# Attention block with projection and feed-forward on one core: weights split ahead of the first rows, the shift rows placed before a store, one GpSimd difference moved, GpSimd's sum added at the next tile, more adds on VectorE in the last item

## The chip, the core and the metric

The kernel runs on one core of one Trainium2 chip. The metric is the device time of one execution in microseconds (us). PE is TensorE, DVE is VectorE, ACT is ScalarE, POOL is GpSimd and SP is SyncE, which here issues every DMA. The engines run their own instruction streams in order and meet at semaphores.

## What is computed

`x` is 2 x 2048 rows of 256 values in float32. Cut to what matters:

```python
def attn(x, W_qkv, W_out):            # H, D = 16, 64
    q, k, v = split(x @ W_qkv, 3)     # 256 -> 3 * 1024
    score = einsum('bihd,bjhd->bijh', q, k) / D ** 0.5      # causal mask
    out = einsum('bijh,bjhd->bihd', softmax(score, over j), v)
    return out.reshape(b, l, H * D) @ W_out                 # 1024 -> 256

x = x + attn(layernorm(x), W_qkv, W_out)
x = x + layernorm(x) @ (W + up_aux @ lora_up @ lora_down @ down_aux).T + b
```

## The kernel before

Products of float32 data are made from a rounded high part and the rest as a low part, so most products are three matmuls (high by high, low by high, high by low). There are three blocks, one after the other.

**Projection** (`project_qkv`, tensors `a_`). Eight tiles of 512 rows. A tile is normalised on DVE (L439), turned by PE (L282), its high part is copied by ACT (`xt_hi`, L405 for the first tile) and its low part taken by DVE (`xt_lo`, L446). PE then makes 24 groups of six matmuls (L304), emptied in turn by ACT and DVE (L359). The weights come in six parts of 512 columns (`w_raw`, loads L209); ACT makes `w_hi` of a part (`high_part`, L381), DVE `w_lo` (`low_part`, L452). Before the first tile parts 0 and 1 are split, after the first rows; the other parts are split between the groups of the first tile. PE starts the first group when part 0 of `w_lo` and `xt_lo` are there.

**Attention** (`attention`, tensors `b_`, `f_`, `g_`). Sixteen items, each two heads of one batch. An item has 40 slots, one for each pair of a query tile t of 512 and a key block j of 128: tile 0 has slots 0 to 3, tile 1 slots 4 to 11, tile 2 slots 12 to 23, tile 3 slots 24 to 39; the last four of a tile lie on the diagonal and are narrower. For a slot, PE makes scores (L839 subtracts the maximum with the rows of `shift`, L843, L851), ACT the exponentials `probs` (L973), PE the product with V (`o_acc`, L908). PE runs two slots ahead with the scores. During item n, PE also makes chunks of scores for item n+1 in a ring of three banks (L872, L880), DVE takes their row maxima (L1047), and near slot 35 turns them into rows (L1060, L1062, semaphore `max_rows_ready`). SP copies these into `shift` with four small DMAs (`place_max`, L782), and PE waits for them at the first scores of item n+1.

The sums of `probs` are split: POOL adds the early j of a tile into `sum_pool` (L1161), DVE the last full one and the diagonal ones into `sum_dve` (L1073, L1077, L1087), and at the end adds `sum_pool` to it (L1093). The table `LATE_FULL` says how many full slots of each tile DVE adds in the last item; in all other items it is one. PE sums over partitions (`denominators`, L920), ACT copies that to `den_row` (L1002), SP moves it (`invert`, L753), DVE inverts it (L1113), SP sends it through memory (L757) and back as `recip` (L761), POOL multiplies (`normalise`, L1146), SP stores (`store_o`, L746). POOL also makes eight low parts of the next item's K and Q per item (`split_diff`, L723) at the slots of the list `LO_SLOTS`, from copies by ACT at slots 0 to 3 (L959, L961).

In the last item there are no chunks. There SP loads the first outputs (`load_first_o`), ACT and DVE split them (`first_high` L995, `first_low` L1107) and the output weights (L989, L1101).

**Output projection and feed-forward** (`project_and_ffn`, tensors `c_`) is not touched.

The order on each engine is written out by hand: the functions `item` of each engine walk through the slots. `late_tile(n, s, previous)` gives the tile that ended just before slot s (s = 0, 4, 12, 24). On SP an item is: load V, invert and store tile 3 of the item before, invert and store tile 0, then for p = 0, 1 a load, invert and store of tile p + 1, then `place_max`.

## Time and profile before

| | us |
|---|---|
| median of 3 runs | 1861.03 |
| lowest and highest run | 1859.17, 1866.96 |
| the profiled execution | 1860.62 |
| its span, from first to last instruction | 1858.8 |
| projection / attention / rest, from the span's start | 0 to 313 / 313 to 1713.7 / to 1858.8 |

In the profile a row of the order in time gives the start in us from the span's start, the length in us, engine, line, operation, output <- inputs, and how many instructions are merged (x4); in brackets stands how long the engine was idle just before and what released it. Rows of waits give: engine, line, what it waited for: us in total, times, longest.

### The profile page before, as it was taken

What the parts mean: (1) busy time and instruction counts of PE and PEld (TensorE: products, weight loads), DVE (VectorE), ACT (ScalarE), POOL (GpSimd) and SP (SyncE); (2) the same over time, 40 slices, a digit from 0 to 9 for tenths busy, and PEclk for the clock granted to TensorE, in tenths of its full rate; (3) what the DMA queues carried; (4) which work ended last, traced back from release to release, by engine and by line L of the source; (5) the groups of instructions that cost most, each with busy time, mean ns of one, the idle gap of its engine ahead of it and who ended that gap; (6) DMA issues with size and microseconds to landing.
All of it is one profiled execution on the core that took longest, in us unless ns stands there. A gap on an engine that the chain in (4) does not pass through costs nothing. (4 is left out here: it accounts for less than half of the span.)

```text
span 1858.8 us, 34889 instructions
## 1 busy us (share of the span) xinstructions
PE 1774.3 (95%) x13720; PEld 1051.1 (57%) x13720; DVE 1243.1 (67%) x2094; ACT 788.2 (42%) x982; POOL 958.7 (52%) x529
## 2 busy tenths in 40 slices
PE   7999999999999999999999999999999999999998
PEld 5878777554545454445454455445454545444897
DVE  5365653767676767676767767676767676756665
ACT  3222114454545454545454454545454545455231
POOL 1011001666665858485766656666667585835211
PEclk9999999999999999999999999999999999999999
DMA  5656446212121212122121222121212121022551
GB/s 209 223 184 233 164 176 215 69 42 75 47 69 48 72 50 69 47 69 73 49 70 47 78 59 78 41 81 36 81 47 70 47 75 47 24 75 92 193 204 57
DMA packets 153858, 171.39 MB, mean 92 GB/s; under 512 B 48202, under 2 KB 94816, under 8 KB 153696
## 3 DMA queue, kind: packets, MB, share of 16 engines
q1 hardware_dynamic: 153696, 169.17, 28.7%
q8 instruction: 110, 1.80, 0.4%
q14 instruction: 52, 0.43, 0.1%
HBM read 97.02 MB, written 71.57 MB: 91 GB/s over the span
## 5 line engine op out<-in xcount | busy, mean ns | idle before, releaser
L1047 DVE TENSOR_REDUCE f_part_max<-b_ring 128x1 f32<-128x512 f32 (+3 forms) x1200 | 675.0, 604 | 289.2 <-PE b_ring L872 193.3
L973 ACT ACTIVATE b_probs<-b_scores 128x1024 f32<-128x1024 f32 (+3 forms) x640 | 564.3, 898 | 604.0 <-PE b_scores L843 343.1
L1161 POOL TENSOR_TENSOR b_sum_pool<-b_sum_pool,b_probs 128x1024 f32<-128x1024 f32 x234 | 558.9, 2388 | 31.8 <-POOL b_sum_pool L1161 0.5
L843 PE MATMUL b_scores<-b_split 64*128 64x512 f32 (+2 forms) x1920 | 296.8, 418 | 0.0
L843 PE MATMUL b_scores<-f_split 64*128 64x512 f32 (+2 forms) x1920 | 295.9, 416 | 0.0
L1161 POOL TENSOR_TENSOR b_sum_pool<-b_probs 128x1024 f32<-128x1024 f32 x48 | 114.6, 2387 | 314.3 <-DVE g_sum_dve L1093 204.4
L908 PE MATMUL b_o_acc<-b_probs,b_v_in 128*64 128x512 f32 (+3 forms) x1280 | 271.2, 545 | 0.0
L908 PE MATMUL b_o_acc<-b_probs,f_v_in 128*64 128x512 f32 (+3 forms) x1280 | 269.0, 541 | 0.0
L843 PEld LDWEIGHTS b_scores<-b_split 64*128 64x128 f32 x1920 | 179.7, 189 | 12.0
L843 PEld LDWEIGHTS b_scores<-f_split 64*128 64x128 f32 x1920 | 179.5, 188 | 11.2
L1087 DVE TENSOR_TENSOR g_sum_dve<-g_sum_dve,b_probs 128x512 f32<-128x512 f32 (+3 forms) x198 | 158.1, 798 | 31.0 <-ACT b_probs L973 26.5
L872 PE MATMUL b_ring<-b_split 64*128 64x512 f32 (+2 forms) x640 | 142.8, 434 | 18.9 <-DVE f_part_max L1047 18.0
L359 DVE COPY a_stage_d<-a_made 128x512 f32<-128x512 f32 x96 | 66.1, 690 | 140.5 <-PE a_made L304 140.4
L359 ACT COPY a_stage_a<-a_made 128x512 f32<-128x512 f32 x96 | 56.4, 587 | 224.6 <-PE a_made L304 222.9
L908 PEld LDWEIGHTS b_o_acc<-b_probs,b_v_in 128*64 128x64 f32 x1280 | 78.2, 137 | 110.4 <-issue 81.5
L872 PE MATMUL b_ring<-f_split 64*128 64x512 f32 (+2 forms) x560 | 125.1, 434 | 16.1 <-DVE f_part_max L1047 15.4
L908 PEld LDWEIGHTS b_o_acc<-b_probs,f_v_in 128*64 128x64 f32 x1280 | 77.6, 136 | 107.9 <-issue 80.5
L872 PEld LDWEIGHTS b_ring<-b_split 64*128 64x128 f32 x640 | 64.7, 183 | 129.1 <-issue 124.6
L839 PE MATMUL b_scores<-b_shift,p_first_rows 64*128 64x512 bf16 (+2 forms) x640 | 117.9, 358 | 10.9 <-ACT b_probs L973 6.6
L839 PE MATMUL b_scores<-f_shift,p_first_rows 64*128 64x512 bf16 (+2 forms) x640 | 117.4, 356 | 9.6 <-ACT b_probs L973 5.3
L872 PEld LDWEIGHTS b_ring<-f_split 64*128 64x128 f32 x560 | 56.7, 184 | 112.2 <-issue 107.7
L723 POOL TENSOR_TENSOR b_split<-f_raw,b_split 128x512 fp32r<-128x512 f32 x64 | 81.4, 1295 | 54.4 <-ACT b_split L959 54.4
(138 smaller groups left out, 2208.8 us busy)
## 6 DMA issues: line engine op xcount, KB each, us to landing
f_raw<-k_t SPq DMA_DIRECT2D x32, 512.0 KB, 4.7
f_raw<-q_t SPq DMA_DIRECT2D x32, 512.0 KB, 5.8
g_recip<-r_t SPq DMA_DIRECT2D x128, 128.0 KB, 2.9
o_t<-g_o_norm SPq DMA_DIRECT2D x64, 256.0 KB, 2.0
q_t<-a_stage_a SPq DMA_DIRECT2D x32, 256.0 KB, 2.4
q_t<-a_stage_d SPq DMA_DIRECT2D x32, 256.0 KB, 2.0
k_t<-a_stage_a SPq DMA_DIRECT2D x32, 256.0 KB, 2.0
k_t<-a_stage_d SPq DMA_DIRECT2D x32, 256.0 KB, 2.0
```

What stands on the lines that cost most here:

```text
L359: copy(stage[e][s][:], made[:, g % BANKS, :]).then_inc(emptied[e], 1)
L723: vec.tensor_tensor(lo[u][:, cols], raw[p][:, which, inner], halves(hi[u][:, cols]), ALU.subtract).then_inc(split_lo, 1)
L839: nc.tensor.matmul(scores[s % 2][:, h, lo:TILE], consts["first_rows"][head(h), :], shift[u][head(h), queries], start=True, stop=False)
L843: last = nc.tensor.matmul(scores[s % 2][:, h, lo:TILE], a[u][head(h), keys], b[u][head(h), queries], start=False, stop=(term == 2 and not ...
L872: last = nc.tensor.matmul(rowwise[h][:, 0:wide], q_hi[u][head(h), ib * P:(ib + 1) * P], k_hi[u][head(h), c * TILE:c * TILE + wide], start= ...
L908: last = nc.tensor.matmul(o_acc[head(h), off:], v_in[u][:, j, head(h)], probs[s % PR][:, h, off:], start=(j == 0), stop=(j == NB * t + NB ...
L973: nc.scalar.activation(probs[s % PR][:, :, off:], scores[s % 2][:, :, off:], ACT.Exp, scale=scale).then_inc(exp_done, 1)
L1047: nc.vector.tensor_reduce(part_max[:, h, ib, c:c + 1], rowwise[h][:, 0:width], AX.X, ALU.max).then_inc(chunk_reduced, 1)
L1087: nc.vector.tensor_tensor(sum_dve[t % 2][:, :, off:], sum_dve[t % 2][:, :, off:], probs[s % PR][:, :, off:], ALU.add).then_inc(dve_added, 1)
L1161: nc.gpsimd.tensor_tensor(sum_pool[:], first, probs[s % PR][:], ALU.add).then_inc(pool_added, 1)
```

## The change

Five edits:

- **First rows.** ACT makes `w_hi` of parts 0 and 1 before `xt_hi` of the first tile, DVE `w_lo` of parts 0 and 1 before `xt_lo`. PE starts the first group at `xt_hi`, and waits for `xt_lo` only ahead of its third matmul.
- **Placing.** `place_max` on SP stands before the store of tile 2 rather than after it.
- **LO_SLOTS.** The second difference moves from slot 8 to 3, the third to fifth from 9, 10, 11 to 8, 9, 10, and the first from 3 to 2.
- **The sum of POOL** (L1093) is issued by DVE at the slot after the tile, ahead of that slot's own add, not behind the last add of the tile.
- **LATE_FULL** goes from (0, 1, 2, 6) to (0, 2, 4, 6): in the last item DVE adds one full slot more of tile 1 and two more of tile 2, and POOL as many less.

```diff
@@ TensorE, group() and tile() of the projection
+                            if first and (g, k) == (0, 2):
+                                pe.wait_ge(xt_lo_ready, 1)
...
-                    pe.wait_ge(xt_lo_ready, T + 1)
+                    if first:
+                        pe.wait_ge(xt_hi_ready, 1)
+                    else:
+                        pe.wait_ge(xt_lo_ready, T + 1)
@@ ScalarE
                 take_root(0, 0)
+                for p in range(2):
+                    high_part(p)
                 act.wait_ge(transposed, 1)
                 nc.scalar.copy(xt_hi[0][:], turned[:]).then_inc(xt_hi_ready, 1)
-                for p in range(2):
-                    high_part(p)
@@ VectorE
                 normalise(0, 0)
+                for p in range(2):
+                    low_part(p)
                 turn(0, 0)
...
-                for p in range(2):
-                    low_part(p)
@@ attention
-    LO_SLOTS = [3, 8, 9, 10, 11, 20, 21, 22]
+    LO_SLOTS = [2, 3, 8, 9, 10, 20, 21, 22]
...
-    LATE_FULL = (0, 1, 2, 6)
+    LATE_FULL = (0, 2, 4, 6)
@@ SyncE
                         invert(n, p + 1)
+                        if following and p == LOADS - 1:
+                            place_max(n + 1, 1 - u)
                         store_o(n, (pair, u), p + 1)
-                    if following:
-                        place_max(n + 1, 1 - u)
@@ VectorE
-                    if d == NB - 1 and first_dve(n, t) < NB * t:
-
-                        dve.wait_ge(dve_added, dve_before[n, s] + 1)
-                        dve.wait_ge(pool_added, pool_done[n, t])
-                        nc.vector.tensor_tensor(sum_dve[t % 2][:], sum_dve[t % 2][:], sum_pool[:], ALU.add
-                                                ).then_inc(dve_added, 1)
+                def add_pool_sum(n, t):
+
+                    dve.wait_ge(dve_added, sum_ready[n, t] - 1)
+                    dve.wait_ge(pool_added, pool_done[n, t])
+                    nc.vector.tensor_tensor(sum_dve[t % 2][:], sum_dve[t % 2][:], sum_pool[:], ALU.add).then_inc(dve_added, 1)
...
+                        for late in late_tile(n, s, previous):
+                            if late[1]:
+                                add_pool_sum(*late)
                         if dve_adds(n, s):
                             add_unit(n, s)
```

What the change moves is seen in the order of instructions. Names in it are output<-inputs; [waits ...] are the semaphores. First ACT at the start of the program, before and now:

```order
2 L370 ACTIVATE a_root<-a_var_eps 128x4 [waits a_var_ready]
3 L405 CAST a_xt_hi<-a_turned 128x1024 [waits a_transposed]
4 L381 CAST a_w_hi<-a_w_raw 128x2x512 [waits a_w_loaded0]
5 L381 CAST a_w_hi<-a_w_raw 128x2x512 [waits a_w_loaded1]
6 L381 CAST a_w_hi<-a_w_raw 128x2x512 [waits a_w_loaded2]
```

```order
2 L375 ACTIVATE a_root<-a_var_eps 128x4 [waits a_var_ready]
3 L386 CAST a_w_hi<-a_w_raw 128x2x512 [waits a_w_loaded0]
4 L386 CAST a_w_hi<-a_w_raw 128x2x512 [waits a_w_loaded1]
5 L412 CAST a_xt_hi<-a_turned 128x1024 [waits a_transposed]
6 L386 CAST a_w_hi<-a_w_raw 128x2x512 [waits a_w_loaded2]
```

Two parts of the weights moved ahead of the first rows; on DVE the same two parts moved ahead of `xt_lo`.

Then SP near the end of the first item, from the loads of `recip` for tile 2 on, before and now:

```order
239 L761 DMA g_recip<-r_t 64x512 [waits g_inverse_stored,g_o_stored]
240 L761 DMA g_recip<-r_t 64x512
241 L746 DMA o_t<-g_o_norm 128x512 [waits g_o_ready,g_o_stored]
242 L782 DMA b_shift<-f_max_high 1x16x128 [waits f_max_rows_ready,f_shift_cleared]
243 L782 DMA b_shift<-f_max_low 1x16x128
```

```order
239 L766 DMA g_recip<-r_t 64x512 [waits g_inverse_stored,g_o_stored]
240 L766 DMA g_recip<-r_t 64x512
241 L787 DMA b_shift<-f_max_high 1x16x128 [waits f_max_rows_ready,f_shift_cleared]
242 L787 DMA b_shift<-f_max_low 1x16x128
243 L787 DMA b_shift<-f_max_high 1x16x128
244 L787 DMA b_shift<-f_max_low 1x16x128
245 L751 DMA o_t<-g_o_norm 128x512 [waits g_o_ready,g_o_stored]
```

The store went behind the four placing DMAs, in each of 15 items.

Last DVE in tile 2 of the last item, between the sums of POOL of tile 1 and tile 2, before and now:

```order
1852 L1093 TENSOR_TENSOR g_sum_dve<-g_sum_dve,b_sum_pool 128x1024 [waits b_pool_added,g_dve_added]
1853 L1107 TENSOR_TENSOR f_split<-f_raw,f_split 128x1024 [waits g_o_hi_ready] x2
1854 L1113 RECIPROCAL g_recip_spread<-g_den_spread 128x8 [waits g_den_moved]
1855 L1073 TENSOR_TENSOR g_sum_dve<-b_probs 128x1024 [waits b_exp_done]
1856 L1107 TENSOR_TENSOR f_split<-f_raw,f_split 128x1024 [waits g_o_hi_ready]
1857 L1087 TENSOR_TENSOR g_sum_dve<-g_sum_dve,b_probs 128x1024 [waits g_dve_added,b_exp_done]
1858 L1087 TENSOR_TENSOR g_sum_dve<-g_sum_dve,b_probs 128x2x384 [waits g_dve_added,b_exp_done]
1859 L1087 TENSOR_TENSOR g_sum_dve<-g_sum_dve,b_probs 128x2x256 [waits g_dve_added,b_exp_done]
1860 L1107 TENSOR_TENSOR f_split<-f_raw,f_split 128x1024 [waits g_o_hi_ready]
1861 L1087 TENSOR_TENSOR g_sum_dve<-g_sum_dve,b_probs 128x2x128 [waits g_dve_added,b_exp_done]
1862 L1093 TENSOR_TENSOR g_sum_dve<-g_sum_dve,b_sum_pool 128x1024 [waits b_pool_added,g_dve_added]
```

```order
1854 L1099 TENSOR_TENSOR g_sum_dve<-g_sum_dve,b_sum_pool 128x1024 [waits b_pool_added,g_dve_added]
1855 L1112 TENSOR_TENSOR f_split<-f_raw,f_split 128x1024 [waits g_o_hi_ready] x2
1856 L1078 TENSOR_TENSOR g_sum_dve<-b_probs 128x1024 [waits b_exp_done]
1857 L1118 RECIPROCAL g_recip_spread<-g_den_spread 128x8 [waits g_den_moved]
1858 L1092 TENSOR_TENSOR g_sum_dve<-g_sum_dve,b_probs 128x1024 [waits g_dve_added,b_exp_done] x2
1859 L1112 TENSOR_TENSOR f_split<-f_raw,f_split 128x1024 [waits g_o_hi_ready]
1860 L1092 TENSOR_TENSOR g_sum_dve<-g_sum_dve,b_probs 128x1024 [waits g_dve_added,b_exp_done]
1861 L1092 TENSOR_TENSOR g_sum_dve<-g_sum_dve,b_probs 128x2x384 [waits g_dve_added,b_exp_done]
1862 L1092 TENSOR_TENSOR g_sum_dve<-g_sum_dve,b_probs 128x2x256 [waits g_dve_added,b_exp_done]
1863 L1112 TENSOR_TENSOR f_split<-f_raw,f_split 128x1024 [waits g_o_hi_ready]
1864 L1092 TENSOR_TENSOR g_sum_dve<-g_sum_dve,b_probs 128x2x128 [waits g_dve_added,b_exp_done]
1865 L1099 TENSOR_TENSOR g_sum_dve<-g_sum_dve,b_sum_pool 128x1024 [waits b_pool_added,g_dve_added]
```

The first add of the tile now stands ahead of the reciprocal, and two adds of full width came in behind it. In the other fifteen items the instructions of DVE stand in the same order as before; on POOL one difference of eight moved from behind a `normalise` to ahead of the adds of tile 1.

## Rows read from the trace of the kernel before

**Rows 1.** The page: busy time of each engine, its share, instructions.

```profile
PE 1774.3 (95%) x13720; PEld 1051.1 (57%) x13720; DVE 1243.1 (67%) x2094; ACT 788.2 (42%) x982; POOL 958.7 (52%) x529
```

**Rows 2.** Waits of PE: who waited for whom, us in total, times, longest.

```profile
PE b_ring L872 <- DVE f_part_max L1047: 33.4, 55, 1.8
PE b_scores L839 <- ACT b_probs L973: 11.9, 18, 2.4
PE b_scores L839 <- issue: 6.8, 15, 1.3
...
PE b_ring L920 <- DVE g_sum_dve L1093: 2.5, 1, 2.5
```

**Rows 3.** In order of time, the start, all engines.

```profile
11.98 1.01 ACT L405 CAST a_xt_hi<-a_turned 128x1024 fp32r<-128x1024 f32 x1 [4.56 <-PE a_turned L282]
12.89 2.94 ACT L381 CAST a_w_hi<-a_w_raw 128x1024 fp32r<-128x1024 f32 x3
13.03 1.23 DVE L446 TENSOR_TENSOR a_xt_lo<-a_turned,a_xt_hi 128x1024 fp32r<-128x1024 f32 x1 [3.17 <-ACT a_xt_hi L405]
...
14.45 3.42 DVE L452 TENSOR_TENSOR a_w_lo<-a_w_raw,a_w_hi 128x1024 fp32r<-128x1024 f32 x3
...
15.71 0.77 PE L304 MATMUL a_made<-a_xt_hi,a_w_hi 128*128 128x512 f32 x1 [3.77 <-issue]
```

**Rows 4.** Line 209, the first two loads of weights, issued from 1.2 us.

```profile
DMA to landing us min/median/max: 4.7/5.0/5.4
```

**Rows 5.** Stretches: length, PE, PEld, DVE, ACT, POOL busy (instructions), clock, DMA share, GB/s.

```profile
15.60:18.70 3.10, 2.99 (x7) 2.44 (x8) 2.27 (x3) 0.28 (x2) 0.00 (x0) 1.00 0.00 0
```

**Rows 6.** In order of time, the end of item 3, first scores of item 4.

```profile
658.50 0.29 DVE L1062 TENSOR_TENSOR f_max_low<-b_ring,f_max_high 128x128 bf16<-128x128 f32 x1
...
658.98 0.33 SPq L746 DMA_DIRECT2D o_t<-g_o_norm  x1
...
661.26 0.59 SPq L782 DMA_DIRECT2D f_shift<-f_max_low  x1
...
663.06 0.39 PE L839 MATMUL b_scores<-f_shift,p_first_rows 64*128 64x512 bf16 x2 [0.22 <-issue]
```

**Rows 7.** In order of time, slots 8 to 13 of item 4, from 663.06.

```profile
684.53 2.30 DVE L1073 TENSOR_TENSOR g_sum_dve<-b_probs 128x1024 f32<-128x1024 f32 x1
...
687.31 0.44 PE L872 MATMUL b_ring<-b_split 64*128 64x384 f32 x2 [1.02 <-DVE f_part_max L1047]
...
688.66 0.20 DVE L1113 RECIPROCAL g_recip_spread<-g_den_spread 128x8 f32<-128x8 f32 x1 [0.31 <-DMA g_den_spread<-g_den_row]
...
693.49 0.49 PE L872 MATMUL b_ring<-b_split 64*128 64x512 f32 x2 [0.63 <-DVE f_part_max L1047]
```

**Rows 8.** The same item, DVE alone, its first chunk.

```profile
672.21 1.29 DVE L1047 TENSOR_REDUCE f_part_max<-b_ring 128x1 f32<-128x512 f32 x2 [2.65 <-PE b_ring L880]
```

**Rows 9.** In order of time, the last item, first gap of PE.

```profile
1645.24 1.10 SPq L761 DMA_DIRECT2D g_recip<-r_t  x2
...
1648.87 2.26 POOL L1146 TENSOR_TENSOR g_o_norm<-g_o_raw,g_recip 128x512 f32<-128x512 f32 x1
...
1657.43 1.04 ACT L995 CAST f_split<-f_raw 128x1024 fp32r<-128x1024 f32 x1 [2.08 <-DMA f_raw<-o_t]
...
1659.45 0.39 PE L839 MATMUL b_scores<-b_shift,p_first_rows 64*128 64x512 bf16 x2 [2.44 <-ACT b_probs L973]
```

**Rows 10.** The page, DMA issues: KB each, median us to landing.

```profile
g_recip<-r_t SPq DMA_DIRECT2D x128, 128.0 KB, 2.9
```

**Rows 11.** In order of time, the last item, second gap of PE.

```profile
1670.03 11.55 POOL L1161 TENSOR_TENSOR b_sum_pool<-b_sum_pool,b_probs 128x1024 f32<-128x1024 f32 x4
...
1679.25 6.16 DVE L1087 TENSOR_TENSOR g_sum_dve<-g_sum_dve,b_probs 128x1024 f32<-128x1024 f32 x3
...
1688.20 1.08 PE L920 MATMUL b_ring<-g_sum_dve,p_ones 128*32 128x256 f32 x8 [2.47 <-DVE g_sum_dve L1093]
```

**Rows 12.** The stretch behind the second gap, columns as in Rows 5.

```profile
1687.90:1691.20 3.30, 3.00 (x20) 1.49 (x20) 0.24 (x1) 0.43 (x2) 2.77 (x2) 0.50 1.01 374
```

More of the change, by code:

```diff
@@ L1137, in _ @@
                     item(n // 2, n % 2, n < LAST_ITEM, n > 0)
+                add_pool_sum(LAST_ITEM, TI - 1)
             @block.gpsimd
```

## The prediction

> **What bounds the kernel now.** First the busy times: PE is busy 95% of the span, the next engine 67% [rows 1]. So a microsecond is won only where PE stands still or runs at its lower clock. Then the waits of PE [rows 2]: 33.4 us at chunks for the ring that DVE empties, in 55 pieces; 11.9 us for exponentials; 6.8 us in 15 pieces at the first scores of an item, released by none of the engines; 2.5 us once at L920. With the start (15.7 us until the first projection matmul, 3.77 of it behind the turning [rows 3]) these are the places that the edits can touch. Matmul ends are modelled: without a wait the next one starts some 0.07 us before the end of the last, so a wait is that much longer than the row says.
>
> **First rows.** Now PE waits for `xt_lo` and `w_lo` of part 0, made by DVE one behind the other: `xt_lo` from 13.03, then three parts of `w_lo` in 3.42 us, 1.14 each, from 14.45; PE starts at 15.71 [rows 3]. ACT stood idle for 4.56 us ahead of 11.98, from 7.42, and DVE for 3.17 ahead of 13.03, from 9.86 [rows 3]. The first two weight loads were issued from 1.2 us and landed in at most 5.4 us [rows 4], so by 7.2. The three `w_hi` parts took 2.94 us [rows 3], 0.98 each: ACT makes two from 7.42 to 9.4, DVE their low parts from 9.9 to 12.2, all in idle time; `xt_hi` still starts at 11.98 (the turning sets it) and ends at 13.0. PE then starts its first two matmuls at 13.05 and waits for `xt_lo`, which still ends at 14.26. The third matmul now begins at 14.3; before, it came two matmuls behind 15.71. In the stretch behind the start seven matmuls took 3.0 us, 0.43 each [rows 5]: the lower level, 1.2 GHz, although the column of the clock reads 1.00 there (its first record lies at 18.7 us; later matmuls follow each other every 0.23 us). So the third matmul was due at 15.71 + 0.14 + 2 x 0.43 = 16.7, and the gain is 2.4 us if the clock rises as much sooner. If it rises at 18.7 all the same, the 2.4 us won are spent at the lower level and are worth half, 1.2. PE's early work is broken by a wait of about 0.4 us, so I take 2.0. Nothing later is due sooner than it comes: `w_lo` of part 2 follows at about 15.8 and is needed at the ninth group. ACT's part 2 starts where it did.
>
> **Placing.** In all 15 boundaries the chain is the same: the second row of maxima ready, the store of tile 2, four placing DMAs of about 0.63 us each, and PE starts when the last has landed. In the row: ready at 658.79, store issued at 658.98, last placing at 661.26 (so the first at 659.40), PE at 663.06, 0.22 us late [rows 6]. Placing first starts it when SP sees the rows: at the earliest at 658.79, at the latest about when SP now issues the store; 0.42 to 0.61 sooner, I take 0.5. Twelve of the 15 gaps are 0.21 to 0.46 and vanish; three (0.87, 1.21, 1.34: a placing DMA itself was issued over 1 us or 1.5 us long) lose 0.5 each. From the total of 6.8 [rows 2] the three make 3.4, so 3.4 + 1.5, and 0.07 for 7 or 8 of them at least: 5.4. If the long issues belong to the store ahead, all of 6.8 + 15 x 0.07 = 7.8 goes. The store is 2.4 us later, and nothing waits for it: the next step on SP is the load of V, held until the next item. What is late next is the exponential of slot 38, done a microsecond before. The chains behind the boundary (denominators, reciprocals) start from PE and move with it.
>
> **LO_SLOTS.** The difference that leaves slot 11 was the fifth; POOL ran it against the first add of tile 1 on DVE, which took 2.30 us in item 4 against 1.14 for an op of that width; the gap of PE at the chunk behind it is 1.02 [rows 7]. It looks like a gain of 0.2 to 1 an item, 7 us in all (gaps there of 14 items). But DVE then waits 0.31 for the transfer of the denominators, and PE stands again at 693.49 for DVE [rows 7]; DVE is busy without a break between the two. That transfer is issued behind a store that waits for POOL's `normalise`, and ahead of `normalise` stand three differences before and three now. So DVE would only wait longer at 688.66, and PE resumes at 693.49 as before: 0 is taken, -7 is the bound. The difference that comes to slot 3 runs beside two narrow adds; DVE has 2.65 us idle ahead of the first chunk of the item [rows 8], which covers one collision (2.30 - 1.14 = 1.2).
>
> **POOL's sum.** Tiles end at slots 12, 24 and 0, and no chunk is planned for the first place of these slots, so nothing stands between the old and the new position: 0. (The order of DVE shows it.)
>
> **LATE_FULL, tile 1.** PE's first gap in the last item, 2.44 us, ends with an exponential that ACT runs behind `first_high`, which waited 2.08 for a load of o_t [rows 9]. That load waits for the store behind `normalise`, 1648.87 to 1651.13 [rows 9]. One POOL add less ends POOL 2.4 us or more sooner, but the loads of `recip` were issued at 1645.24 and 1645.8 and take 2.9 [rows 9, 10], so they land at 1648.7: the start stays. Only its length, 2.26, may shrink toward 1.3 as DVE has less to collide with. 0 to 2.4, I take 0.5.
>
> **LATE_FULL, tile 2.** The second gap, 2.47 us, is PE at L920 waiting for POOL's sum on DVE, which ended at 1688.15; PE had been there since 1685.7 [rows 11]. POOL made five adds, four of them in 11.55 us to 1681.6; now three, over by about 1675. DVE's three adds took 6.16, 2.05 each beside POOL [rows 11], against 1.14 alone. The new chain behind the reciprocal at 1673.3: three wide adds, two splits, 1.14 to 1.23 each, narrower ones of 0.96, 0.68, 0.42, and the sum of 1.23: 9.6 us, so 1683, and 1685 with two collisions: in time for 1685.7. Behind the gap the granted clock was 0.50 for 3.3 us [rows 12], the lower level: half of it, 1.7, is lost. So 2.47 + 1.7 = 4.2; 4.0 is taken. The upper bound of the cost: all adds at 2.05 and one split at 3.4 as then, two adds more than before, the first add (2.6) out of the chain: 4.1 - 2.6 = +1.5.
>
> **Sum.** -2.0 - 5.4 - 0 - 0 - 0.5 - 4.0 = -11.9. Against the profiled execution's 1860.62 this gives 1848.7. That execution lies 0.4 us under the median of the three, 1861.03, so it stands for them.
>
> **Rivals.** (a) *The collision was the cause.* PE's gaps near slot 9 go: -7 more, 1841.7. For it: the longest of these gaps go with the longest adds. Against: the wait for the denominators between [rows 7].
> (b) *Given back.* The 5.4 us of the boundaries return at the next wait, the exponentials 4 us on (0.56 each in [rows 2]) or the ring: 1854.1. Against: these chains start from PE's own scores.
> (c) *The adds block each other.* In tile 2 DVE stays late and the half clock stays: 1848.7 + 4.0 + 1.5 = 1854.2. For it: 2.05 us an add in [rows 11]. The Trainium skill ("SBUF — State Buffer", Who interferes with whom) says that a VectorE instruction with two SBUF inputs and a GpSimd instruction that reads SBUF exclude each other for a whole instruction; by that rule the trace agrees in kind (2.30 against 1.14), and each add moved to VectorE is one more to be blocked. Against: POOL is through with its three adds before most of them.
> (d) *Slower.* The difference at slot 3 delays the first chunk reduction in each item, and PE runs into the ring: it decides once the delay passes the cover of 2.65 us; past it one collision, 1.2 us, for 15 items costs 17.4: 1866.1. One collision alone stays inside the cover, so it needs three.
>
> **How the numbers follow.** Chances: the forecast 0.57, (a) 0.14, (b) 0.11, (c) 0.14, (d) 0.04. The time is that of the forecast. The terms' own bounds give 1848.7 + 0.8 + 0.5 + 0.5 + 1 = 1851.5 on one side and 1848.7 - 0.4 - 2.4 - 1.9 = 1844.0 on the other. With (a), (b) and (c) the range is 1840 to 1856. About 0.5%, 9.3 us, is what a measurement of this kernel can tell from no change (its three runs lie 7.8 us apart). Under 1851.7 lie nearly all of the forecast and (a): faster 0.68; (b), (c) and the rest within 0.5%: 0.29; slower 0.03.
>
> **What would show it.** Right: third projection matmul at 14.3; first scores of an item released without a gap in most of 15 boundaries, the total of that wait under 2 us; the first add of tile 1 near 1.3 us in every item, yet the gaps of PE at slots 8 to 13 unchanged in sum; L920 in the last item without a wait, one stretch of half clock less. Wrong: DVE's first reduction of an item with less than 1 us idle ahead of it; PE's first gap in the last item gone; gaps at slots 8 to 13 gone (rival a).

## The result and the profile after

The changed kernel took 1851.5 us (median of 10 runs, 1847.6 to 1856.6) beside 1863.5 us of the kernel before on the same chip (10 runs): a ratio of 0.9939, 95% interval 0.9927 to 0.9951, or 11.4 us less (9.1 to 13.6). The forecast was 11.9 less, as an absolute time 1848.7 us with a range of 1840 to 1856. The profiled executions have spans of 1858.8 and 1846.5 us, 12.3 apart. Where the 12.3 lie, from the first scores of the items:

| stretch | before | after | difference | forecast for what is edited in it |
|---|---|---|---|---|
| start to first scores of item 0 | 313.1 | 312.4 | -0.7 | -2.0 |
| items 0 to 14 | 1320.0 | 1313.1 | -6.9 | -5.4 |
| last item and all behind it | 225.8 | 221.0 | -4.8 | -4.5 |

These are two single executions, and the clock differs between them: the record of the granted clock has half clock for 3.4 us in items 0 to 14 before and for 6.8 us after, and behind them for 10.5 us before (3.7 of it behind attention) and for 0.8 after. So the last row is flattered and the middle one isn't; more on both below.

The busy times, from the page of the changed kernel; PE's work is the same as in [rows 1], the span around it shorter:

```profile
PE 1774.2 (96%) x13720; PEld 1048.5 (57%) x13720; DVE 1243.4 (67%) x2097; ACT 788.2 (43%) x982; POOL 945.1 (51%) x526
```

The waits of PE in the changed kernel (who waited for whom, us in total, times, longest), against [rows 2]:

```profile
PE b_ring L877 <- DVE f_part_max L1052: 30.1, 45, 1.9
PE b_scores L844 <- ACT b_probs L978: 11.5, 18, 2.0
...
PE b_ring L925 <- DVE g_sum_dve L1099: 1.3, 1, 1.3
...
PE b_scores L844 <- issue: 0.9, 3, 0.5
```

The wait at the first scores of an item went from 6.8 us in 15 pieces to 0.9 in 3. The ring wait went from 33.4 us in 55 pieces to 30.1 in 45, its longest from 1.8 to 1.9.

**The start**, in order of time, all engines, against [rows 3]:

```profile
9.78 2.35 DVE L457 TENSOR_TENSOR a_w_lo<-a_w_raw,a_w_hi 128x1024 fp32r<-128x1024 f32 x2
...
11.98 1.01 ACT L412 CAST a_xt_hi<-a_turned 128x1024 fp32r<-128x1024 f32 x1 [2.68 <-PE a_turned L282]
...
13.05 0.79 PE L306 MATMUL a_made<-a_xt_hi,a_w_hi 128*128 128x512 f32 x1 [1.10 <-ACT a_xt_hi L412]
...
14.30 0.79 PE L306 MATMUL a_made<-a_xt_lo,a_w_hi 128*128 128x512 f32 x1
...
14.90 0.63 PE L306 MATMUL a_made<-a_xt_hi,a_w_hi 128*128 128x512 f32 x1
```

Every time is the one worked out: `w_lo` inside DVE's idle time, PE at 13.05, the third matmul at 14.30 instead of 16.70. But of these 2.4 us only 0.7 are left at the first scores of this execution.

**A boundary**, the end of item 3 and the first scores of item 4, in order of time, against [rows 6]:

```profile
656.88 0.29 DVE L1067 TENSOR_TENSOR f_max_low<-b_ring,f_max_high 128x128 bf16<-128x128 f32 x1
...
657.24 0.55 SPq L787 DMA_DIRECT2D f_shift<-f_max_high  x1
...
659.10 0.59 SPq L787 DMA_DIRECT2D f_shift<-f_max_low  x1
...
659.79 0.53 SPq L751 DMA_DIRECT2D o_t<-g_o_norm  x1
...
661.16 0.39 PE L844 MATMUL b_scores<-f_shift,p_first_rows 64*128 64x512 bf16 x2
```

The rows of maxima are ready at 657.17; the first placing DMA goes 0.07 us later (before, 0.6 later), and PE has no gap.

**Slots 8 to 13 of item 4**, DVE alone, against [rows 7]; the item begins at 661.16:

```profile
682.63 1.22 DVE L1078 TENSOR_TENSOR g_sum_dve<-b_probs 128x1024 f32<-128x1024 f32 x1
683.77 0.75 DVE L1052 TENSOR_REDUCE f_part_max<-b_ring 128x1 f32<-128x256 f32 x2
684.43 0.95 DVE L1092 TENSOR_TENSOR g_sum_dve<-g_sum_dve,b_probs 128x768 f32<-128x768 f32 x1
687.81 0.20 DVE L1118 RECIPROCAL g_recip_spread<-g_den_spread 128x8 f32<-128x8 f32 x1 [2.43 <-DMA g_den_spread<-g_den_row]
687.93 0.97 DVE L1052 TENSOR_REDUCE f_part_max<-b_ring 128x1 f32<-128x384 f32 x2
```

SP and PE in the same stretch of the changed kernel:

```profile
682.82 0.34 SPq L751 DMA_DIRECT2D o_t<-g_o_norm  x1
683.25 2.39 SPq L758 DMA_DIRECT2D g_den_spread<-g_den_row  x4
```

```profile
688.58 0.76 PE L877 MATMUL b_ring<-b_split 64*128 64x512 f32 x2 [1.90 <-DVE f_part_max L1052]
```

The add that took 2.30 us takes 1.22. In exchange DVE waits 2.43 us, not 0.31, for the denominators, and PE stands 1.90 us where it stood 1.02 and 0.63. Behind this gap lies a stretch at half clock, here with the columns of [rows 5]; the column of the clock reads 0.58 over 4 us:

```profile
688.00:692.00 4.00, 3.42 (x16) 2.04 (x18) 3.97 (x8) 0.58 (x1) 0.00 (x0) 0.58 0.07 8
```

**The last item**, the three gaps of PE, and what ACT, DVE and POOL did for the third, against [rows 9] and [rows 11]:

```profile
1650.57 0.39 PE L844 MATMUL b_scores<-b_shift,p_first_rows 64*128 64x512 bf16 x2 [1.10 <-ACT b_probs L978]
1654.84 0.64 PE L925 MATMUL b_ring<-g_sum_dve,p_ones 128*32 128x256 f32 x8 [1.31 <-DVE g_sum_dve L1099]
1666.18 0.34 PE L844 MATMUL b_scores<-b_shift,p_first_rows 64*128 64x384 bf16 x2 [2.00 <-ACT b_probs L978]
```

```profile
1641.33 1.27 POOL L1155 TENSOR_TENSOR g_o_norm<-g_o_raw,g_recip 128x512 f32<-128x512 f32 x1 [3.30 <-DMA g_recip<-r_t]
...
1652.22 0.20 DVE L1118 RECIPROCAL g_recip_spread<-g_den_spread 128x8 f32<-128x8 f32 x1 [7.47 <-DMA g_den_spread<-g_den_row]
...
1664.16 1.04 ACT L1000 CAST f_split<-f_raw 128x1024 fp32r<-128x1024 f32 x1 [2.79 <-DMA f_raw<-o_t]
...
1676.54 1.22 DVE L1099 TENSOR_TENSOR g_sum_dve<-g_sum_dve,b_sum_pool 128x1024 f32<-128x1024 f32 x1
```

POOL's sum of tile 2 is added by 1677.8 and L925 doesn't wait there. The gaps of this item, 2.44 + 2.47 = 4.9 us before, are now 1.10 + 1.31 + 2.00 = 4.4: they moved more than they shrank. What went are the two stretches of half clock at them (from 1660.54 and 1687.85), 3.41 us each in the record of the clock, half of it lost: 2 x 1.7. The item, from its first scores to the first projection matmul behind attention, went from 80.7 to 77.0 us. The other 1.1 of the 4.8 lies behind attention, where nothing was edited: the kernel before has a half-clock stretch at 1728.81 there and the changed one has none.

### The profile page after: what moved, and what is told of

It reads as the page before. It is cut to its first block and busy times, and to the rows that moved or that the text cites. A ratio compares the mean times of both kernels' runs of the same rounds, so it can differ in the third digit from the quotient of the medians.

```text
span 1846.5 us, 34889 instructions
## 1 busy us (share of the span) xinstructions
PE 1774.2 (96%) x13720; PEld 1048.5 (57%) x13720; DVE 1243.4 (67%) x2097; ACT 788.2 (43%) x982; POOL 945.1 (51%) x526
## 5 line engine op out<-in xcount | busy, mean ns | idle before, releaser
L1170 POOL TENSOR_TENSOR b_sum_pool<-b_sum_pool,b_probs 128x1024 f32<-128x1024 f32 x231 | 549.4, 2378 | 31.3 <-POOL b_sum_pool L1170 0.5
L1092 DVE TENSOR_TENSOR g_sum_dve<-g_sum_dve,b_probs 128x768 f32<-128x768 f32 (+3 forms) x201 | 173.7, 864 | 30.4 <-ACT b_probs L978 25.3
```

The costliest lines, as they stand in the source:

```text
L1092: nc.vector.tensor_tensor(sum_dve[t % 2][:, :, off:], sum_dve[t % 2][:, :, off:], probs[s % PR][:, :, off:], ALU.add).then_inc(dve_added, 1)
L1170: nc.gpsimd.tensor_tensor(sum_pool[:], first, probs[s % PR][:], ALU.add).then_inc(pool_added, 1)
```

## The experiments

Each was timed in five rounds against the kernel before on the same chip. Differences in us come from the ratio and the median of the kernel before that was timed beside it (1860.9 us for the first four kernels, 1860.7 for the next four, 1862.4 for the last four). Two sums over a profiled execution are used throughout: the *add time*, DVE's first add of tile 1 summed over 15 items, and the *gap time*, PE's gaps at the ring in the stretch 17 to 33 us behind an item's first scores, summed over the same items, the shortest gaps too. Before: 26.0 and 19.7 us. After: 19.4 and 19.6. The gap time scatters by some 3 us from one execution to the next: in the six kernels that leave both LO_SLOTS and the late denominators as they were it is 19.7, 20.0, 20.6, 22.1, 22.6 and 22.7.

### Each edit alone

**The start edit alone:** the hunks of TensorE, ScalarE and the first of VectorE from the diff.

> The kernel before with the first edit alone: weights of parts 0 and 1 split ahead of the first rows, PE starts at xt_hi and waits for xt_lo ahead of its third matmul. In the changed kernel's trace the third matmul came at 14.30 as forecast, but the full clock only at 19.65 instead of 18.73, and attention began 0.7 us sooner, not 2.0. Theory A (what this edit is worth hangs on when the clock rises in the execution): attention begins 0.3 to 2.4 us sooner than the 313.08 of the kernel before, the difference explained by the time at which the clock row begins; the total by 0.7 to 2 us, too little to be told. Rival B (the broken start holds the clock down each time): 0.7 us every time, the clock rises near 19.6. A groups gap elsewhere in the projection: none expected.

Measured: ratio 0.9995 [0.9978, 1.0012], -0.9 us (-4.1 to +2.2). The timing can't tell this from nothing. The first scores came at 311.4 us; what that number says is taken up below, with the twelfth run.

**The placing alone:**

```diff
+                        if following and p == LOADS - 1:
+                            place_max(n + 1, 1 - u)
                         store_o(n, (pair, u), p + 1)
-                    if following:
-                        place_max(n + 1, 1 - u)
```

> The kernel before with place_max ahead of the store of tile 2 alone. Theory: the first scores of an item lose their wait of 6.8 us in 15 pieces down to under 1.5, the fifteen items from 399 to 1633 us shorten by 5 to 7 us together, total -5 to -7 us (ratio 0.9965). Rival (given back at the next wait, exponentials or ring): items shorten by under 2 us, total ratio 0.999 to 1.

Measured: 0.9960 [0.9943, 0.9976], -7.4 us (-10.6 to -4.5). Its wait at the first scores:

```profile
PE b_scores L839 <- issue: 0.7, 2, 0.4
```

Items 0 to 14 took 1314.7 us, 5.3 less than before. Over all kernels with late denominators, the three with this edit take 1313.1, 1313.2 and 1314.7 us for these items, the five without it 1318.3 to 1322.2: 7.2 less on average. This one edit carries two thirds of the result. The wait went almost as a whole. Three placing DMAs are still issued slowly, but for 0.76, 1.16 and 1.28 us where it was 1.20, 1.50 and 1.60; why they are shorter isn't known.

**LO_SLOTS alone:**

```diff
-    LO_SLOTS = [3, 8, 9, 10, 11, 20, 21, 22]
+    LO_SLOTS = [2, 3, 8, 9, 10, 20, 21, 22]
```

> The kernel before with LO_SLOTS changed alone. Theory: the first add of tile 1 on DVE takes 1.2 to 1.3 us in all items instead of up to 2.3, but DVE then waits longer for the denominators' transfer, and the wait of PE for the ring keeps its sum (33 us) within 2; total ratio 0.999 to 1.001. Rival (the collision was the cause): the ring waits fall by 5 to 7 us, total ratio 0.9965.

Measured: 1.0014 [1.0001, 1.0027], +2.6 us (+0.2 to +5.0), gap time 21.1 us. DVE's wait for the denominators (us in total, times, longest), first in the kernel before, then here:

```profile
DVE g_recip_spread L1113 <- DMA g_den_spread<-g_den_row: 42.5, 32, 6.5
```

```profile
DVE g_recip_spread L1113 <- DMA g_den_spread<-g_den_row: 54.5, 31, 8.2
```

The adds became shorter by 6.1 us in sum (19.9, not 26.0) and the wait longer by 12.0: nothing is won. Rival (a) of the prediction, that the collision of POOL's difference with DVE's first add of tile 1 was the cause, is refuted: taking it away alone doesn't close the gaps.

**LATE_FULL alone:**

```diff
-    LATE_FULL = (0, 1, 2, 6)
+    LATE_FULL = (0, 2, 4, 6)
```

> The kernel before with LATE_FULL = (0, 2, 4, 6) alone, the sum of POOL where it was. Theory from the changed kernel's trace: the wait of 2.47 us at L920 in tile 2 goes and the half clock behind it too, but new waits come (1.3 us at L920 of tile 1, 2.0 at an exponential in tile 2 behind a split that waits for a load); the last item takes 77 us instead of 80.7; total -3 to -4 us (ratio 0.998). Rival (forecast): 4.5 us from the last item, with only the first gap left. Rival 2: nothing, the gaps only move and the last item keeps its 80.7.

Measured: 0.9988 [0.9977, 0.9999], -2.2 us (-4.3 to -0.2), a little under the 3 to 4 expected. In its trace the last item has gaps of 1.35, 1.06 and 1.61 us (4.0 in all), no half clock in it, and from its first scores to the end it takes 224.4 us, 1.4 less than before: two half-clock stretches more lie behind attention. The item itself takes 77.1 us, as in the changed kernel (77.0) and not 80.7. This kernel has the sum of POOL at its old place, so nothing of the last item's gain needs the new place.

Together the four come to -7.9 us beside -11.4 for the whole. The intervals of the four added in squares give about 5.4 us either way, so this is no sign that the parts help each other.

### What holds slots 8 to 13

The theory from here on: the reciprocal of tile 0 on DVE waits for its denominators, and the ring's reductions are queued behind it. These denominators are late because SP issues them behind the store of the previous item's tile 3, and that store waits for POOL's `normalise` (682.74 its end, 682.82 the store, 683.25 the loads, in the rows of SP above; the store came at 684.59 in the kernel before, 21.5 us into the item, and at 682.82 here, 21.7 into it).

**The loads of `den_spread` of tile 0 ahead of the store**, in the changed kernel:

```diff
                         invert(n - 1, TI - 1)
+                        spread(n, 0)
                         store_o(n - 1, (pair - 1 + u, 1 - u), TI - 1)
...
-                    invert(n, 0)
+                    invert(n, 0, not previous)
```

`spread` is the first half of `invert`: its four loads, whose wait is left as it was.

> The changed kernel, and beside it SP issues the four den_spread loads of tile 0 of an item ahead of the store of the previous item's tile 3, not behind it. Theory: in slots 8 to 13 of every item PE stops because DVE's reciprocal of tile 0 (2.43 us of waiting for the denominators in the item from 661.16 of the changed kernel) holds the reductions of the ring behind it; with the denominators there in time that wait of DVE is under 0.5 us, the waits of PE on f_part_max fall from 30.1 us to 14 to 20, and the time is 8 to 14 us under the changed kernel: ratio to the kernel before 0.986 to 0.990. Rival: DVE's own work in these slots sets the pace, the reciprocal merely fills a hole; the waits of PE stay at 28 us or more and the ratio at 0.993 to 0.995. Second rival: the store of tile 3 comes later by the four loads and delays what waits for it; the ratio is 0.995 or more.

Measured: 0.9818 [0.9801, 0.9836], 1827.3 us: 33.9 under the kernel before, and 22.5 under the changed one by the ratios, more than the 8 to 14 expected. The mechanism was forecast, its worth too low. SP and then DVE of its item 4:

```profile
673.78 2.46 SPq L758 DMA_DIRECT2D g_den_spread<-g_den_row  x4
677.47 0.34 SPq L751 DMA_DIRECT2D o_t<-g_o_norm  x1
```

```profile
677.43 1.22 DVE L1083 TENSOR_TENSOR g_sum_dve<-b_probs 128x1024 f32<-128x1024 f32 x1
678.57 0.75 DVE L1057 TENSOR_REDUCE f_part_max<-b_ring 128x1 f32<-128x256 f32 x2
679.23 0.95 DVE L1097 TENSOR_TENSOR g_sum_dve<-g_sum_dve,b_probs 128x768 f32<-128x768 f32 x1
680.10 0.20 DVE L1123 RECIPROCAL g_recip_spread<-g_den_spread 128x8 f32<-128x8 f32 x1
680.21 0.97 DVE L1057 TENSOR_REDUCE f_part_max<-b_ring 128x1 f32<-128x384 f32 x2
```

The same five instructions as in the changed kernel, without the 2.43 us ahead of the reciprocal. Gap time 6.8 us, not 19.6, none longer than 0.36. Waits in this kernel, of PE and of DVE:

```profile
PE b_ring L882 <- DVE f_part_max L1057: 19.8, 38, 0.9
```

```profile
DVE g_recip_spread L1123 <- DMA g_den_spread<-g_den_row: 24.5, 16, 7.7
```

Fifteen of 31 waits for denominators are gone, those of tile 0. Items 0 to 14 took 1295.9 us, 17.2 less than in the changed kernel. 12.8 of them are gap time and 1.7 the half clock behind the gap of 1.90; the remaining 2.7 I can't place (the other half-clock stretch of the changed kernel, at 313.19, cost little: its item 0 took 85.9 us beside 85.7 here).

**The reciprocal later**, at slot 11 instead of 9, in the changed kernel with the loads where they were:

```diff
-                        for late in late_tile(n, s - 5, previous):
+                        for late in late_tile(n, s - (7 if s == 11 else 5), previous) if s != 9 else []:
                             reciprocals(*late)
```

> The changed kernel with DVE's reciprocal of tile 0 two slots later (slot 11, not 9), nothing else moved. If the landing of the denominators is what stops DVE in slots 8 to 13, its wait there falls from 2.4 us to under 0.5 and the waits of PE on f_part_max fall by 8 us or more as when the loads come sooner: ratio 0.986 to 0.991, less what the later loads of recip and the later normalise cost. If the loads were not the limit, nothing moves: 0.993 to 0.995. If the later normalise of tile 0 holds POOL's adds, it is slower than the changed kernel: 0.996 or more.

Measured: 0.9843 [0.9825, 0.9862], 1829.2 us, a little more gain than expected; gap time 6.6, add time 18.3. Here DVE comes to the same wait later, with the same effect. This excludes that SP's new order itself, or the store behind it, brought the gain.

**Both together:**

> The changed kernel with both: the loads of den_spread of tile 0 ahead of the store of tile 3 and DVE's reciprocal of it at slot 11, not 9. Each alone gave 0.982 and 0.984. Theory: both take away one and the same wait, so together they give no more than the better one: 0.980 to 0.983. Rival: the loads alone left some of the wait (24.5 us in 16 times over the whole program) in front of the reductions, and the later reciprocal takes it too: 0.977 to 0.979.

Measured: 0.9825 [0.9806, 0.9844], 1829.9 us; gap time 6.6. No more than either alone: it is one wait.

### LO_SLOTS with the wait and without

**The changed kernel with the old LO_SLOTS:**

> The changed kernel with LO_SLOTS as before. Alone, the new LO_SLOTS gave a ratio of 1.0014 [1.0001, 1.0027]. If the sooner difference costs the same beside the other edits, this kernel is 2 to 3 us under the changed one: ratio 0.992 to 0.993. If the new slots pay only beside the earlier placing, it is 2 to 4 us over it: ratio 0.995 to 0.996. If the table does nothing, 0.994.

Measured: 0.9920 [0.9901, 0.9939], -14.9 us. Gap time 22.1 and items 0 to 14 in 1313.2 us, as in the changed kernel (1313.1). The timing leans to the old table as it did with LO_SLOTS alone, by 3.5 us, but the intervals touch, and no row shows where it would come from. In the last item and behind it this kernel takes 225.9 us, with the new LATE_FULL, beside 225.8 of the kernel before.

**The same with the loads ahead of the store:**

> The changed kernel with the den_spread loads of tile 0 ahead of the store of tile 3 and LO_SLOTS as before. Theory: the sooner differences brought nothing alone (ratio 1.0014) and nothing beside the other edits, since DVE's reciprocal waited for the denominators either way. With that wait gone the collision of POOL's difference with DVE's first add of tile 1 (2.30 us for an add of 1.22) is no longer covered, and the old table costs 1 us an item: 8 to 15 us over the kernel with the loads alone, ratio 0.986 to 0.990. Rival: the table does nothing here either, ratio 0.980 to 0.983.

Measured: 0.9851 [0.9830, 0.9871], -27.7 us. DVE's add in item 4, 2.06 us long:

```profile
679.94 2.06 DVE L1083 TENSOR_TENSOR g_sum_dve<-b_probs 128x1024 f32<-128x1024 f32 x1
```

Add time 24.6 and gap time 13.6, against 18.7 and 6.8 with the new table: 5.9 us longer adds, 6.8 us more gaps, and 6.2 us by the ratios (about 5 either way), under the 8 to 15 expected.

**The kernel before with the loads ahead of the store,** none of the five edits:

> The kernel before with the den_spread loads of tile 0 ahead of the store of tile 3, none of the five edits of the change. If the loads and the change add up, their gain is the ratio of the kernel with both to the changed one, 0.9818 / 0.9939 = 0.988: 1838 us. If the old LO_SLOTS keep the first add of tile 1 colliding, and this replaces the wait removed, the gain is under half of that: ratio 0.994 to 1.000.

Measured: 0.9927 [0.9910, 0.9945], -13.6 us; add time 25.0, gap time 13.8. My second case said that under half of the gain would be left, and the first that all of it would. It is between: 13.6 of 22.5. In its trace 10.0 us of this lie in items 0 to 14 and 3.8 in the last item and behind it: there PE's gap at L925 is 0.68 us, where it was 2.47, with the old LATE_FULL, and the item takes 76.9 us. So once the denominators come early, the new LATE_FULL has little left to give.

The kernels side by side, us against the kernel before, with gap time behind it:

| | old LO_SLOTS | new LO_SLOTS |
|---|---|---|
| none of the other edits, denominators late | 0 (19.7) | +2.6 (21.1) |
| none of the other edits, denominators early | -13.6 (13.8) | not run |
| the other edits, denominators late | -14.9 (22.1) | -11.4 (19.6) |
| the other edits, denominators early | -27.7 (13.6) | -33.9 (6.8) |

So the collision and the late denominators are two causes of one gap, and the later of them sets it. Remove the collision alone and nothing comes; remove the wait alone and 13 us come; remove both and another 6 come.

The traces show the collision in detail. The add of width 1024 takes 1.22 us where POOL runs nothing beside it. In the kernel before that is so in item 0 alone. In the 14 other items a POOL instruction is under way when the first add of tile 1 begins, and each time the add takes 1.08 us plus what was left of that instruction (0.46 to 1.23 us), within 0.01: it stands still until POOL is through. In items 2 and 5 that instruction is `normalise`; a difference then begins while the add is under way, and now it is the difference that takes 2.25 us, not 1.27. The new LO_SLOTS move only differences, and the collisions with `normalise` remain (1.95 and 1.57 us in items 2 and 5 of the changed kernel). The Trainium skill ("SBUF — State Buffer", Who interferes with whom) says that a VectorE instruction with two SBUF inputs and a GpSimd instruction that reads SBUF shut each other out; by that rule the trace agrees, with these lengths.

### The parts of the last item

**With the loads early, the reads of `o_t` later:**

```diff
-        PART_SLOTS = [12 + 3 * p for p in range(PARTS)]
+        PART_SLOTS = [14, 17, 22, 25]
```

> As the kernel with the den_spread loads ahead of the store of tile 3, and the reads of o_t for the first projection's parts in slots 14, 17, 22 and 25 of the last item, not 12, 15, 18 and 21. Theory: the waits of 1.3 and 2.0 us in the last item of the changed kernel are behind the splits of f_raw that ACT and DVE wait for; with the parts later they go, and the time is 2 to 3 us under the kernel with the loads alone. Rival: the parts are then late at the end of the last item, and what is won is given back at the first matmuls behind attention: the same time as with the loads alone, within 1 us.

Measured: 0.9824 [0.9807, 0.9840], 1828.1 us, the same as without it. The gap at the exponential is gone (2.54 us with the loads alone), and these two stand instead, in the last item and right behind it:

```profile
1654.98 0.64 PE L930 MATMUL b_ring<-g_sum_dve,p_ones 128*32 128x256 f32 x8 [1.28 <-DVE g_sum_dve L1104]
...
1680.08 0.47 PE L1354 MATMUL c_y<-g_wo_hi,f_split 128*128 128x256 f32 x2 [2.00 <-DVEq L1494]
```

The second was 1.09 with the loads alone. From the last item's first scores on it is 222.2 us beside 221.4: the rival was right, what is won comes back at the first matmul behind attention.

### The start, and what the clock does

**Weights first, but PE still waiting for `xt_lo`:** the start edit without the hunks of TensorE, in the kernel before (an unbroken start; with the edit whole, PE stops again ahead of its third matmul).

> The kernel before with the first two parts of the weights split while the first rows are turned, PE still waiting for xt_lo ahead of its first matmul (unbroken start near 14.3 us). The first scores of item 0 come at 311.4 to 312.4 us where PE starts at 13.05 and stops for xt_lo, against 313.1 to 314.4 in the kernel before. If the start at xt_hi buys nothing, since the third matmul stands at 14.3 either way, they come at the same place less 0.1 (two matmuls of half clock, 0.8 us at most, are behind the wait instead of ahead of it, so 0.4 to 0.8 later at equal clock). If the broken start holds the full clock back, they come sooner than with it by 0.5 or more. Ratio 0.999 either way.

Measured: 0.9986 [0.9973, 0.9999], -2.6 us (-5.0 to -0.2). PE, in order of time:

```profile
14.33 0.79 PE L304 MATMUL a_made<-a_xt_hi,a_w_hi 128*128 128x512 f32 x1 [2.36 <-DVE a_xt_lo L446]
14.92 0.63 PE L304 MATMUL a_made<-a_xt_hi,a_w_lo 128*128 128x512 f32 x1
15.35 0.63 PE L304 MATMUL a_made<-a_xt_lo,a_w_hi 128*128 128x512 f32 x1
```

The twelve kernels of the experiments, the kernel before and the changed one have only three kinds of start. For each the time at which the record of the clock first shows full speed, and the first scores:

| start | full clock from, us | first scores, us |
|---|---|---|
| as before (15.71) | 18.62, 18.73, 18.85, 21.46, 21.55 | 313.07, 313.08, 313.15, 314.35, 314.42 |
| changed (13.05, then 14.30) | 16.73, 16.87, 17.67, 18.09, 18.13, 19.13, 19.28, 19.65 | 310.96, 311.02, 311.38, 311.62, 311.64, 312.09, 312.22, 312.39 |
| unbroken (14.33) | 19.89 | 312.98 |

Kernels with the same start see the clock rise up to 2.9 us apart, and each microsecond of that moves the first scores by half a microsecond, as it should between 1.2 and 2.4 GHz. So two executions don't compare until this is taken out, in one of two ways. On average over the executions shown the clock rose at 19.8 us with the old start and at 18.2 with the new, and the first scores came at 313.6 and 311.7: a difference of 1.9 us. At one and the same rise, 18.7 us, they come at 313.1 and 311.9: 1.2 us of it, the two and a half microseconds of earlier work done at half speed; the other 0.8 is the mean rise, 1.6 us sooner. The pair of before and after caught an early rise for the old start (18.73) and the latest of eight for the new (19.65), and so shows 0.7. The unbroken start, with one execution, comes at 312.4 at the same rise: 0.7 from the weights, and 0.5 more from starting at `xt_hi`. That the broken start holds the full clock back, as the profile of the changed kernel alone seemed to say, is not so: with the same start it also came at 16.73. The rises scatter by 1.1 to 1.5 us (standard deviation), so averages over five and eight executions leave the 1.9 open by about 0.8 us, and by themselves don't show that the rise on average comes sooner; the 1.2 at an equal rise doesn't hang on that.

## Why the prediction was right, and where not

**The start** was forecast at -2.0, between 1.2 if the clock rises at 18.7 all the same and 2.4 if it rises as much sooner. Over thirteen executions it is worth 1.2 at an equal rise, and 1.9, within about 0.8, on average, so the step holds as far as they can tell, though for another reason than the one given: not the short wait in PE's early work decides between the ends, but when the clock rises in that execution. The single pair of traces shows 0.7, outside both ends, and would have misled without the others.

**Placing** was forecast at -5.4, up to -7.8. Alone it measured -7.4, and the stretch of items fell by 6.9. The mechanism was the one described and the term too small: I gave the three gaps with a long issue a gain of only 0.5 us each, which leaves 1.9 us of wait, and 0.9 is left, since the long issues became shorter. It was not given back (rival (b)): the wait for exponentials went from 11.9 to 11.5.

**LO_SLOTS** at 0 was right in mechanism; in size it came out at 0 or slightly worse (+2.6 us alone, 3.5 beside the other edits, the first just clear of noise and the second not). "PE resumes as before" holds in the sum: gap time 19.7 and 19.6, though with a scatter of some 3 us the closeness of this pair is luck. The first add of tile 1 did come down, to 1.22 us in 13 of 15 items. I had named the link that the runs then showed to be the cause (the transfer behind a store behind `normalise`), but priced only its standing still, not what its removal would be worth. The difference at slot 3 does run into an add, which takes 1.37 us instead of 0.69, but there is 1.96 us idle left ahead of the first chunk of the item (2.65 in [rows 8]), so rival (d) stayed away. DVE in the changed kernel, item 4:

```profile
666.97 1.37 DVE L1092 TENSOR_TENSOR g_sum_dve<-g_sum_dve,b_probs 128x512 f32<-128x512 f32 x1 [0.50 <-ACT b_probs L978]
670.31 1.29 DVE L1052 TENSOR_REDUCE f_part_max<-b_ring 128x1 f32<-128x512 f32 x2 [1.96 <-PE b_ring L885]
```

**POOL's sum** at 0: it was not run alone, but the last item takes 77.1 us with LATE_FULL and the old place and 77.0 with the new.

**LATE_FULL** was forecast at -4.5. The -4.8 of the pair of traces only seems to confirm it: 3.7 lie in the item, the rest behind attention. Alone the edit measured -2.2, and the last item says the same over all kernels with late denominators: 80.7, 79.8, 79.7, 79.2 and 79.2 us with the old table, 77.0, 77.1 and 78.5 with the new, 2.2 less on average. So this term was mis-sized by a factor of two. For tile 1 the step held to the row: POOL's `normalise` starts 15.8 us into the item as before (1641.33 - 1625.51, 1648.87 - 1633.05) and only its length falls, 2.26 to 1.27, and with it the gap, 2.44 to 1.10. L925 in tile 2 is reached without a wait, by the chain that the prediction added up (1683 forecast for a gap that ended at 1688; here 1677.8 with items shifted by 7.5, so 1685 on the old scale, 2 us later than forecast and still in time). But the 2.47 us of that gap weren't won: a wait of 2.00 came at the exponential 10 us ahead, behind a split that waits for `o_t`, which I had not looked at for tile 2, and 1.31 at L925 of tile 1, since DVE's adds there stand behind a reciprocal that waits 7.47 us for its denominators. And the credit of 1.7 us for the half clock depends on the execution: the changed kernel has none in the last item, and one at 688.66 and one at 313.19 that the kernel before has not, while that has one at 779.90 and one at 1728.81 that the changed one has not. The third kernel with the new table and late denominators has a half-clock stretch at 1666.72 in the last item, and of the old ones only the kernel before has two there, the others one. Rival (c) asked for DVE to stay late in tile 2; it was in time.

So the sum of -11.9 met -11.4 partly by luck: placing was up to 2 us better than its term, LATE_FULL some 2 worse, LO_SLOTS perhaps 3 worse, and the start can't be told better than within a microsecond.

## What to carry to other kernels

Where an engine waits a little behind a long operation, ask what that operation hides: here an add slowed by GpSimd and a transfer that landed at the same time ended in one gap, and shortening the add alone brought nothing, while moving the transfer alone brought 13 us and both 19. SP issues its DMAs in program order, which puts every store's wait in front of the loads behind it, so loads whose data are ready go ahead of a store that waits for a slow engine. And before a row of one pair of profiles is credited to an edit, compare the clock records and the same stretch in other kernels: here the pair shows 4.8 us for an edit worth 2.2 alone. The edit worth most here, four issues moved past one store, is not in the change at all.

## What was not expected of the hardware

- The granted clock rises at a time of its own: 16.7 to 19.7 us with one and the same start of the program, 18.6 to 21.6 with another.
- It falls to half behind a single gap of 1.90 us (688.66 in the changed kernel) but not behind one of 2.00 (1666.18). Over all traces it fell behind a gap of 1.68 us (ended at 686.63, in the changed kernel with the old LO_SLOTS) and not behind one of 2.45 (ended at 1661.76, in the kernel with LO_SLOTS alone). So a gap's price is its length or its length and up to 1.7 us, by the execution. Where PE had time to spare the half clock cost less: behind the first scores of item 0, at 312.8 to 313.4, at most 0.4 us.
- The issue of a store to HBM takes SP 0.34 to 0.53 us and that of a placing DMA 0.55 to 0.6, so four placing DMAs take 2.4 us of queue, and the last starts 1.86 us behind the first (657.24 to 659.10). It lands 1.7 us behind its issue, so half of a boundary is the issuing. A few such issues took 1.06 to 1.60 us, in the kernel before and in the changed one.
